# Row maxima of the second attention from 64 rows of TensorE instead of 128

## The reference, cut to what matters

```python
q = q * c + _rot_half(q) * sn
k = k * c + _rot_half(k) * sn
k = jnp.repeat(k, rep, axis=1)          # 16 query heads on 4 key heads
scores = jnp.einsum('bhqd,bhkd->bhqk', q, k) / jnp.sqrt(HD)   # HD = 64
scores = scores + causal_bias
attn = jax.nn.softmax(scores, axis=-1)
```

## Time and profile before

| | |
|---|---|
| median of 3 runs | 3292.73 us (3292.18 to 3293.93) |
| the profiled execution | 3282.75 us, its span 3280.9 us |
| TensorE busy | 3071.8 us, 94% of the span |
| VectorE, ScalarE, GpSimd busy | 79%, 66%, 61% |
| TensorE's granted clock, mean | 0.982 of full |

### The profile page before, as it was taken

One profiled execution on the slowest core, in us unless ns is written; L12 is line 12 of the kernel. 1 busy time (PEld: TensorE's weight loads), 2 busy tenths in 40 slices (PEclk: granted clock), 3 DMA queues, 4 the chain that ended last, 5 costly groups with the idle time before them and its releaser, 6 DMA issues. The chain is left out here.

```text
span 3280.9 us, 50730 instructions
## 1 busy us (share of the span) xinstructions
PE 3071.8 (94%) x16864; PEld 2036.3 (62%) x16864; DVE 2605.9 (79%) x3764; ACT 2173.9 (66%) x4011; POOL 2014.9 (61%) x1573
## 2 busy tenths in 40 slices
PE   5999999799999999999999999999999999999998
PEld 3555555456666577666665776666657766666576
DVE  7788876678888678888886778888867888888677
ACT  4566667676666676766666767666667676666675
POOL 2100000377878676778776757787767677877675
PEclk8899999889999999999999999999999999999999
DMA  5442421323323065323230653233206532332053
GB/s 122 74 77 49 82 61 38 81 71 80 72 68 75 18 196 146 88 63 77 68 73 20 196 142 90 65 75 71 65 24 191 150 89 65 76 71 65 24 185 113
DMA packets 160402, 283.55 MB, mean 86 GB/s; under 512 B 32593, under 2 KB 64209, under 8 KB 159889
## 3 DMA queue, kind: packets, MB, share of 16 engines
q1 hardware_dynamic: 159632, 280.18, 33.9%
q10 hardware_dynamic: 512, 0.13, 0.0%
HBM read 88.47 MB, written 31.72 MB: 37 GB/s over the span
## 5 line engine op out<-in xcount | busy, mean ns | idle before, releaser
L1471 ACT ACTIVATE prob<-psA 128x512 f32<-128x512 f32 x1152 | 658.3, 593 | 510.7 <-PE psA L1869 328.4
L1273 POOL TENSOR_TENSOR xw<-xw,prob 128x512 f32<-128x512 f32 x672 | 872.4, 1298 | 169.3 <-ACT prob L1471 102.3
L2193 DVE TENSOR_REDUCE mxp<-psA 128x1 f32<-128x512 f32 (+3 forms) x864 | 527.6, 663 | 60.2 <-PE psA L1838 59.5
L2167 DVE RECIPROCAL rden<-psA 128x256 f32<-128x256 f32 x256 | 448.5, 1752 | 150.9 <-PE psA L1897 148.4
L1868 PE MATMUL psA<-qs,ks 128*128 128x512 f32 x1152 | 504.4, 438 | 14.3 <-ACT prob L1471 7.9
L1838 PE MATMUL psA<-ks,qs 128*128 128x512 f32 (+3 forms) x1536 | 438.4, 368 | 41.3 <-DVE ks L2295 16.8
L1273 POOL TENSOR_TENSOR xw<-prob 128x512 f32<-128x512 f32 x224 | 288.1, 1286 | 275.4 <-issue 169.9
L1869 PE MATMUL psA<-qs,ks 128*128 128x512 f32 x1152 | 454.1, 394 | 0.0
L1307 POOL TENSOR_TENSOR hidl<-gate,hidh 128x512 fp32r<-128x512 f32 x256 | 335.6, 1322 | 175.0 <-ACT hidh L1549 172.8
L1483 ACT ACTIVATE psA<-maskq 128x512 f32<-128x512 bf16 (+1 forms) x672 | 359.5, 556 | 82.5 <-DVE mxp L2193 55.5
L2115 DVE TENSOR_REDUCE mxp<-psA 128x1 f32<-128x1024 f32 x256 | 304.8, 1220 | 82.8 <-PE psA L1669 81.7
(11 more groups left out here) (222 smaller groups left out, 5855.6 us busy)
## 6 DMA issues: line engine op xcount, KB each, us to landing
qs<-normed SPq DMA_DIRECT2D x256, 256.0 KB, 4.2
rbp<-rab SPq DMA_DIRECT2D x256, 192.0 KB, 3.4
spread<-routing_weights SPq DMA_DIRECT2D x128, 256.0 KB, 3.6
qs<-qs SPq DMA_DIRECT2D x64, 256.0 KB, 3.9
expert_weight_halves<-eh SPq DMA_DIRECT2D x32, 384.0 KB, 3.7
expert_weight_halves<-el SPq DMA_DIRECT2D x32, 384.0 KB, 4.5
eh<-expert_weight_halves SPq DMA_DIRECT2D x32, 384.0 KB, 3.4
el<-expert_weight_halves SPq DMA_DIRECT2D x32, 384.0 KB, 4.1
```

The source lines that it names most:

```text
L1273: g.tensor_tensor(psum_k[:, t % 2, :], before, prob[:, i % 4, :], ALU.add).then_inc(s_su, 1 if kt > 1 else 2 + (t == 1))
L1471: act(prob[:, k % 4, :], psS[:, k % 2, :], ACT.Exp, scale=float(HD) ** -0.5).then_inc(s_ex, 1)
L2167: vec.reciprocal(rden[:, :], psO[t % 2][:, 256:512]).then_inc(s_rd, 1)
L2193: vec.tensor_reduce(dst, bank, AX.X, ALU.max).then_inc(s_mr, 1)
```

## The change

Items M read 64 rows instead of 128: high part of the queries against high part of the keys only. Piece number `m` of a query tile uses the lower 64 rows (`qs1` lower, `ks[:, 0]` lower) when `m` is even and the upper 64 (`qs1` upper, `ks[:, 1]` upper, the copy) when it is odd. The product with the keys' low part is left out of the maxima; the scores that go into the exponential keep it. Number, shapes and waits of the instructions are the same, and nothing else changes.

```diff
                 masked = diagonal(t, m) and seed is None
+                side = m % 2
+                rows = slice(side * HD, (side + 1) * HD)
                 for i in range(w):
-                    ins = mm(bank[:, i, :], qs1[b][:, c, h + i, t % TPC * P:(t % TPC + 1) * P], ks[b][:, 0, k0:k1],
+                    ins = mm(bank[:, i, :], qs1[b][rows, c, h + i, t % TPC * P:(t % TPC + 1) * P], ks[b][rows, side, k0:k1],
                              start=(i == 0 and seed is None), stop=not masked, skip_group_check=True)
```

## The result

The changed kernel takes 3387.58 us (median of 4 runs, 3383.64 to 3389.24), the kernel before beside it 3293.33 us: ratio 1.0285, 95% interval 1.0273 to 1.0298. It is 94 us slower; 113 were forecast, and the time lies in the range of 3300 to 3480. In all that follows, medians leave out two executions of one kernel (the groups beside V) in which the granted clock stood low throughout (mean 0.87 and 0.675).

A forecast was written before the change was run, and what follows sets the result against it. TensorE was taken to bound the kernel: 222 us of added changes less 70 saved by pairs gave 152, less 39 hidden left 113. Added to 3292.7 us this made 3406 us, 3.4% slower, range 3300 to 3480.

The forecast's parts named there:

- TensorE sets the pace in the phases: Attention phases: TensorE busy 468 of 487 us, so what is added to its queue is paid nearly in full.
- The price, 0.09 + 0.11 us a change, read off V and D: Between full array and 64 rows: 0.09 to 0.10 us emptying plus 0.11 us uncovered weight load, 0.20 us each change.
- The rival that going there is free: Going to 64 rows and back costs nothing, leaving only the pairs' gain: 3238 us, faster; chance 0.15.
- that of half the price: At each change the array empties or weights load uncovered, not both: 3324 us; chance 0.12.
- J, the hint for the first: Transpose on 16 columns before S: its starts, 0.57 us together, show no stop, hinting that changes are free.
- The pair costs one matmul: Two M on different sides run together; 360 pairs save 70 us of TensorE.
- 222 - 70 = 152 us on TensorE: TensorE's queue: 1110 more changes at 0.20 us add 222 us, pairs save 70, net 152 us.
- 39 us hidden: Half of TensorE's 67 us of waits in four phases (34 us), plus about 5 between phases, absorbs added time.
- Phases of 509 us, 7 more between them: Profile after: attention phases of about 509 us instead of 488, stretches between them some 7 us longer each.
- Clock: Clock expected at 1.00 in the attention phases; rival that it falls there: about 3600 us, chance 0.03.

The follow-up runs named there:

- the groups beside V: Kernel before, with 64 rows only for the 66 groups of two or more single-matmul M having V or D on at least one side: 3291.62 us, ratio 0.9989.
- one side only: Changed kernel with every M on the lower 64 rows, so no two M can share their time: 3437.16 us, ratio 1.0433.
- The two complementary kernels: Changed kernel with 64 rows kept only for groups of two or more M (3320.98 us), or only for the 304 lone M (3358.25 us); other M use 128.
- the second profile of before: Kernel before, unchanged, profiled once more: span 3292.7 us, mean clock 0.979, 8 falls of the clock in the layers.
- those with another order: Changed kernel, planner treating M as its own kind and a change of kind as 200 ns: 3392.29 us with M on 64 rows, 3377.23 us on 128.
- one more kind in the list: Planner of the changed kernel given M as a kind beside V and D and 200 ns a change, all M on 128 rows: 3377.23 us, ratio 1.0254.

## Why the prediction was right, step by step

- *TensorE sets the pace in the phases*: right. Its added time lengthened them while the other engines' work stayed the same.
- *The price, 0.09 + 0.11 us a change, read off V and D*: right to 0.01 us for rows of the array as for columns (0.31, 0.37 and 0.33 in the timeline; 0.40 for a lone M). The rival that going there is free (0.15) and that of half the price (0.12) are refuted. J, the hint for the first, misled: its 16 columns cost no stop, M's 64 rows do.
- *The pair costs one matmul*: right, 0.003 us between the starts; one side only is 50 us slower. No row of before showed it for row halves, and the prediction inferred it from column halves.
- *222 - 70 = 152 us on TensorE*: not seen as such. The distances around all groups of M grew by 109.5 us, since part of the price fell where TensorE already waited. From S2 to an M behind it the growth is 0.09 us by the median of 418 places, but 0.07 by the mean.
- *39 us hidden*: the term that was mis-sized. By the medians 152 - 94 = 58 were hidden. It was half of TensorE's 67 us of named waits and 5 more, and these 67 us were taken as the bound. The number 58 keeps within it, but it is no bound: the named waits of a phase fell by 5 us only (16.7 to 11.7), 20 in four, and they are read from TensorE's modelled ends, which lie so late that two M whose starts are 0.60 us apart instead of 0.23 leave only 0.11 us of idle time between them. The weight loads of M show more. In the whole span of before, the idle time ahead of them that ScalarE's masks (L1483) ended is 60.6 us; TensorE's own waits name 13.1:

```profile
L1838 PEld LDWEIGHTS psA<-ks,qs 128*128 128x128 f32 x1536 | 260.1, 189 | 171.9 <-issue 60.8 <-ACT psA L1483 60.6 <-DVE mxp L2193 13.4
```

  Where a later TensorE meets such a mask it waits less. The two complementary kernels show that this happens (26 us returned elsewhere with the lone matmuls; groups of three and four M that gain only beside them). How the 58 us divide among the places is not shown.
- *Phases of 509 us, 7 more between them*: 505 to 506 in the last three layers; between the first two 180 against 172 in the second profile of before.
- *Clock*: not the cause of the loss, as forecast (0.99 to 1.00 in the last three phases). It matters only in the experiments, most in those with another order.
- What I didn't have: the profile of before stood 10 us under its median because the clock happened to fall less often (3 times in the layers instead of 8). Adding the difference to the median was right, but a second profile would have told why.

## What to carry to other kernels

A matmul on part of the array is cheap only in company: count the changes of the division in the fixed order of TensorE, both ways, at the price that the trace shows around an existing change, against the matmuls that really run side by side. Here 1115 changes at 0.20 us stood against 360 pairs at 0.2 us, and 304 lone matmuls carried seven tenths of the loss. If an order is planned by costs, give the planner the measured price of a change, and measure again: 200 instead of 110 ns made this kernel 1.0% faster, 300 ns lost it all, and with 200 ns and one more kind in the list it was 83 us slower than before.

## What the runs showed of the hardware beyond that

- Two F32R matmuls of 64 rows and 512 columns on different row halves, into different banks, start 0.003 us apart, and what follows starts 0.432 us behind the first instead of 0.427.
- A transpose of 16 columns between full-array matmuls costs no stop (0.57 us over four starts, 0.58 at all 11 places between S2 and S), 64-row and 64-column products do.
- TensorE's mean granted clock differs between executions of one kernel, 0.975 to 0.981, and its time goes with it, 3300 to 3286 us. On the chip with 17 executions of before the clock accounts for 83% of the variance of the time, on that with 23 for 46%.
- TensorE's named waits can miss what its weight loads show: matmuls that start 0.60 us apart, held by a mask of ScalarE, appear as one row of four without a wait, while two of their weight loads wait 0.41 us each.
